# 16-column attention: the down weights loaded one piece per group, and the last two units of a stage turned into the upper bank of their own scores

## The reference

```
# first of the two: inside the block, x is normalised first, no bias
q, k, v = (x @ w_qkv) split into 12 heads of 16
a = softmax(q @ k.T * 0.25)            # 36 x 36 per image and head
o = (a @ v) merged @ w_proj + b_proj
# the later one
a = softmax(q @ k.T * 0.25 + bias); o = (a @ v) merged @ w_proj.T + b_proj
# the stage behind the first is the MLP (w_fc1, gelu, w_fc2);
# the one behind the later is the mixture of experts (w_gate, w_up, w_down; ws_gate, ws_up, ws_down)
```

## Time and profile before

| | |
|---|---|
| median of 3 runs | 899.25 us (898.99 to 905.46) |
| the profiled execution | 903.05 us, its span 901.3 us |
| TensorE busy | 818.9 us, 91% |
| VectorE | 542.0 us, 60% |
| ScalarE | 439.9 us, 49% |
| GpSimd | 408.7 us, 45% |
| mean granted clock of TensorE | 0.961 |

### The profile page before, as it was taken

The page is one execution under the profiler, slowest core; times in us unless marked ns, Lnnn a source line. Parts: engine busy times, 40 slices in busy tenths (PEclk is TensorE's granted clock), DMA queues, the critical chain, the costliest instruction groups (busy, mean ns, idle before and its releaser), DMA issues. The chain is left out here.

```text
span 901.3 us, 21350 instructions
## 1 busy us (share of the span) xinstructions
PE 818.9 (91%) x7767; PEld 733.5 (81%) x7767; DVE 542.0 (60%) x1467; ACT 439.9 (49%) x1094; POOL 408.7 (45%) x489
## 2 busy tenths in 40 slices
PE   9899999999998898987999989888879999999973
PEld 8889998899997676766999976666657899899973
DVE  2235565556665898993763337788966622467645
ACT  0246555555644576763345527566626221355523
POOL 1534444344444544342442236767841455244444
PEclk9999999999999999996999989898979999999996
DMA  9910111111110232225200013623200111333252
GB/s 308 265 51 21 31 27 37 31 32 30 37 37 2 35 67 26 34 22 172 24 1 1 1 27 50 157 47 65 46 3 2 36 60 63 81 99 107 77 170 94
DMA packets 103942, 55.78 MB, mean 62 GB/s; under 512 B 67264, under 2 KB 94512, under 8 KB 103840
## 3 DMA queue, kind: packets, MB, share of 16 engines
q1 hardware_dynamic: 99248, 45.99, 21.2%
q0 software_dynamic: 3792, 7.84, 2.5%
q10 hardware_dynamic: 800, 0.59, 0.2%
HBM read 29.81 MB, written 13.97 MB: 49 GB/s over the span
## 5 line engine op out<-in xcount | busy, mean ns | idle before, releaser
L931 POOL TENSOR_TENSOR attn_prob<-attn_prob,attn_recip 100x432 f32<-100x432 f32 x64 | 58.6, 916 | 67.1 <-DVE attn_recip L1316 66.6
L450 POOL TENSOR_TENSOR attn_prob_x<-attn_prob,attn_recip 100x864 f32<-100x864 f32 x32 | 52.6, 1644 | 52.8 <-DVE attn_recip L759 52.8
L1892 POOL DMA_INDIRECT results<-moe_hid_shared x43 | 41.1, 955 | 58.1 <-ACT moe_hid_shared L2107 58.1
L1602 ACT ACTIVATE mlp_hid<-psum,columns 128x384 f32<-128x384 f32 x72 | 38.1, 580 | 41.4 <-PE psum L96 41.4
L1047 PE MATMUL psum<-ident,attn_prob 100*108 100x100 f32 x256 | 35.5, 264 | 21.4 <-POOL attn_prob L931 12.9
L1047 PEld LDWEIGHTS psum<-ident,attn_prob 100*108 100x108 f32 x256 | 26.1, 138 | 27.2 <-POOL attn_prob L931 18.7
L1064 PEld LDWEIGHTS psum<-attn_prob_t,attn_values 108*49 108x49 f32 (+1 forms) x1024 | 33.7, 132 | 15.5 <-ACT attn_prob_t L1183 6.7
L1176 ACT ACTIVATE attn_prob<-attn_prob 100x432 f32<-100x432 f32 x64 | 36.1, 564 | 19.0 <-POOL attn_prob L938 17.8
L2082 ACT ACTIVATE moe_silu<-psum 128x384 f32<-128x384 f32 x36 | 17.7, 491 | 56.5 <-PE psum L107 56.5
L1064 PE MATMUL psum<-attn_prob_t,attn_values 108*49 108x36 f32 (+1 forms) x1024 | 36.0, 217 | 8.3 <-DMA attn_values<-attn_v_tok 5.0
L1555 PE MATMUL psum<-mlp_w_dn_s,mlp_hid 128*128 128x192 f32 (+2 forms) x306 | 42.6, 290 | 0.0
(11 more groups left out here) (474 smaller groups left out, 2790.5 us busy)
## 6 DMA issues: line engine op xcount, KB each, us to landing
embed_patches<-in_x SPq DMA_DIRECT2D x8, 768.0 KB, 14.5
sorted_rows<-mlp_pad_zeros SPq DMA_DIRECT2D x1, 4214.0 KB, 15.6
moe_hid_shared<-sorted_rows SPq DMA_DIRECT2D x43, 98.0 KB, 2.1
attn_v<-attn_v_tok SPq DMA_DIRECT2D x16, 216.0 KB
attn_values<-attn_v_tok SPq DMA_DIRECT2D x96, 27.0 KB
side_raw_a<-in_w_gu_dram SPq DMA_DIRECT2D x8, 288.0 KB, 3.2
side_raw_b<-in_w_gu_dram SPq DMA_DIRECT2D x16, 144.0 KB, 3.4
h_rows<-results SPq DMA_DIRECT2D x6, 288.0 KB, 5.4
```

The lines of the kernel that those rows point to most:

```text
L450: nc.gpsimd.tensor_tensor(prob_x[k % 2][:, :, :, :], prob[k % 3][:, :, :].rearrange("p h (a n) -> p h a n", a=1) .to_broadcast([QP, HEADS, ...
L931: nc.gpsimd.tensor_tensor(pr, pr, recip[k % 2][:, :].rearrange("p (h a) -> p h a", a=1) .to_broadcast([QP, HEADS, SEQ]), ALU.mult).then_in ...
L1602: nc.scalar.activation(hid_step(n), bank(n % 3)[:, 0:MW], ACT.Gelu, bias=b_up[:, c:c + 1]).then_inc(S["gelu_done"], 1)
L1892: nc.gpsimd.indirect_dma_start(out=results, out_offset=bass.IndirectOffsetOnAxis(ap=x_in[j % x_ring][:, D:D + 1].bitcast(U32), axis=0), in ...
```

## The change

Two edits. First, the down weights are no longer issued together: piece `n` is issued at `j == 3` behind the value loads and the raw loads of group `n + 2`. Second, the turns of units 30 and 31 write to bank 3 and bank 5, the upper one of the two banks that held their own scores, and no longer wait for `z_copied`; `copy_turned` reads from there. Lines below L863 move down by one or two.

```diff
-    turned_ps = bank(6).rearrange("p (g a n) -> p g a n", g=4, a=2)
+    def turned_bank(k):
+        return bank(6) if k < units - 2 else bank(3 + 2 * (k % 2))
@@ sync
             if side and j == 3 and g + 1 < side.steps:
                 side.load_step(sp, g + 1)
-            if side and k == per_group + 2:
-                side.load_down(sp)
+            if side and j == 3 and 2 <= g < 2 + len(side.loads):
+                side.load_down(sp, g - 2)
@@ turn
             if k >= 1:
                 pe.wait_ge(S["turned_copied"], k)
+            if 1 <= k < units - 2:
                 pe.wait_ge(S["z_copied"], k)
             flat = prob[k % 3][:, :, :].rearrange("p h n -> p (h n)")
             for n in range(4):
-                last = nc.tensor.transpose(bank(6)[0:3 * SEQ, n * P:n * P + QP],
+                last = nc.tensor.transpose(turned_bank(k)[0:3 * SEQ, n * P:n * P + QP],
@@ copy_turned
-            nc.scalar.activation(prob_t[k % 2][:, :, :, :], turned_ps[0:3 * SEQ, :, :, 0:SEQ], ACT.Copy
+            nc.scalar.activation(prob_t[k % 2][:, :, :, :], turned_bank(k).rearrange("p (g a n) -> p g a n", g=4, a=2)[0:3 * SEQ, :, :, 0:SEQ], ACT.Copy
@@ SideWeights
-    def load_down(self, sp):
-        for dst, src in self.loads:
-            sp.dma_start(dst, src).then_inc(self.S["down_loaded"], 16)
+    def load_down(self, sp, n):
+        dst, src = self.loads[n]
+        sp.dma_start(dst, src).then_inc(self.S["down_loaded"], 16)
```

## The result

The changed kernel takes **889.91 us** (median of 5 runs, 889.31 to 890.75), the kernel before 899.25 us beside it (5 runs, 898.85 to 905.46). The ratio is 0.9882, with a 95% interval of 0.9853 to 0.991: between 8 and 13 us less. By the medians it is 9.3 us, 1.04%. In a later comparison on another chip it was 890.34 against 898.29 us, 8.0 us or 0.9%, ratio 0.991 [0.9878, 0.9941].

The account below looks back on a forecast made before the run. The prediction took VectorE as the fuller engine, nearly full at 14.76 of 15.70 us ahead of the stall. Its terms, 5.64 + 0.96 + 0.48 = 7.1 us off 899.25, gave 892.2 us, range 888.5 to 896.5.

Parts of the forecast that it names:

- The stall: Last attention stage, group 2: without down weights ahead, the 3.49 us value wait goes, saving VectorE's idle 5.64 us.
- the move from 903.05 to 899.25 us: Whole kernel: sum made against the profiled execution, then moved down by 3.8 us to the median of three runs.
- The other pieces cost nothing: Last stage, down pieces behind groups 3, 4 and 5: issued in SyncE's idle time, 3.4 us of cover at group 4.
- Two turns of attn2: Earlier stage, last two turns: each no longer waits 0.48 us for the copy of z, 0.96 us saved.
- One turn of attn3: Last stage, second of the last two turns: 0.48 us wait for z saved, dummy matmuls behind it only move along.
- The clock case: Rival, earlier stage's tail: shorter pauses may keep TensorE's clock up, up to 3.1 us more, 889.1 us; chance 0.10.
- Given back: Rival, groups behind the removed stall: one more meeting with GpSimd's work costs 2.8 us, 895.0 us; chance 0.16.
- Stays: Rival, group 2: value loads slow for a reason other than down weights, only turns gain, 897.8 us; chance 0.07.
- slower: Rival, groups 4, 5 and 6: down pieces stall their value loads, 9.8 us more than now, 909.1 us; chance 0.04.
- The forecast's own range: Whole kernel: 890 to 894.5 us if the forecast itself holds, chance 0.63, with 0.2% for a median of three.
- the stated cases: Whole kernel: within 1% chance 0.79, faster by over 1% (below 890.3 us) 0.17, slower by over 1% 0.04.

Follow-up runs that it names:

- e3: Changed kernel, but the four down weights of the later stage issued together behind group 2's value loads; 893.52 us, ratio 0.9947 to the kernel before.
- e1: Kernel before with only the down-weights edit, one piece per group, turns as before; 893.94 us, ratio 0.995.
- e11: Changed kernel, but the down weights issued two and two, behind the value loads of groups 2 and 3; 888.84 us in one run.
- e4: Changed kernel, but the four down weights issued together ahead of group 4's value loads; 887.64 us, ratio 0.9885 to the kernel before.
- e2: Kernel before with only the turns edit, down weights still together ahead of group 2's value loads; 894.31 us, ratio 0.9958.
- e9: Kernel before with the down-weights edit and one dummy matmul in attn3 ahead of unit 31's turn, which still waits for z; 889.81 us in one run.
- e6: Changed kernel with dummy matmuls in the three longest pauses of the tails of both attention stages; 887.43 us, ratio 0.9874 to the kernel before.

## Why the prediction was right, and where it was off

- **The stall.** Mechanism right in each step: value loads issued in 7.5 us, no wait, no low clock, and the price is VectorE's idle time (five profiles, of which e3 excludes the nearest rival). In the profiled pair it is 5.9 us against the 5.64 of the sum. Against the medians the term is too large, since the first profile of before had the dearest stall of three: 4.6 us on the mean, and 4.1 by e1. The step that failed is the move from 903.05 to 899.25 us: it lowered the base by 3.8 us but left the terms as they were, though the stall itself was part of those 3.8.
- **The other pieces cost nothing.** Right: no wait at groups 3 to 6, and e11 shows that even two at once are free. In before, e3 and e4 the big loads had all landed (at the latest 11.0, 10.5 and 11.1 us behind their issue) 3.1 to 3.6 us before the nine value loads were through theirs, and the first mixing follows that issue by 1.3 us with a burst ahead (before, e3, e4) and without (group 0); what e3 and e4 show is the time that the burst holds SyncE and stretches the issue of the loads behind it.
- **Two turns of attn2, 0.96 us.** Right: 0.9 us at like clocks.
- **One turn of attn3, 0.48 us.** This is the term that was mis-sized: 1.7 us. The prediction said that the dummy matmuls behind it only move along. They were shortened as well: the stretch at clock 0.50 ended about 3 us sooner, the four dummy matmuls ahead of mixing 31 took 1.56 us instead of 2.77, and 1.2 us of the 1.7 are that. The tail's clock was not looked at for this turn, though it was for attn2. Why the clock comes back sooner stays open.
- **The clock case,** "more than the sum", gave 889.1 us, nearest to what came, and 889.91 lies below the 890.3 for which the forecast gave a chance of 0.17. Its mechanism did not hold where it was put: the second low stretch in attn2's tail is in one profile of before and absent from two. A clock effect of the edit is there, but in the tail of attn3. That the number came so near is luck.
- **Given back:** no. The waits for GpSimd are 12.9 us in 11 places as before, and the slowest normalisation (L1337 now) takes 3178 ns against 3193. In before five of the 18 take over 1 us, the slowest from 658.49 to 661.68, and each ends 0.11 to 0.12 us behind an unbroken run of GpSimd's instructions (here L938 to L2604, to 661.57). The changed kernel has six, the sixth of 1.12 us, and so has before's second profile. **Stays** and **slower** fell with the first row of SyncE's queue.
- **The forecast's own range,** 890 to 894.5, is narrower than the bounds that it names: 3.5 to 6.8 and 0 to 1.4 us off 899.25 give 891.0 to 895.8, before any noise.
- Together: 4.6 + 0.9 + 1.7 = 7.2 us are traced to the edits, the forecast's 7.1 by other terms; that the sums agree is luck. Measured by the medians are 8.0 and 9.3. From mixing 12 to 20 it is 1.4 us less on the mean, but e2, with the stall, took 32.65 us there, and before itself 32.53 to 35.02. Whether the edits have a part in this stays open. So the gain came out at 0.9 and at 1.0% by the medians of two comparisons (0.9 and 1.2% by the ratios), on the edge between two of the stated cases.

## What to carry to other kernels

Put a stall's price by what the fullest engine behind it loses, not by the wait in the profile; but take it from several executions, because the size of a stall differs from execution to execution (5.9 us in one profile here, 3.6 to 4.3 in three others). When a transfer is late, look at how long the issuing queue was held by what stands ahead: big loads one or two at a time between groups of small ones cost nothing here, four at once cost 3.6 to 5.9 us ahead of group 2 and 2.5 ahead of group 3. Before a short pause is costed at its own length, read the clock behind it until the stage ends.

## What the runs showed of the hardware

- One program takes 890.17 to 903.46 us in 29 runs on one chip, 1.5% apart, its mean clock between 0.960 and 0.975, and time and clock go together (correlation -0.84). The profiles of the same program have their stretches at clock 0.50 at other places and of other lengths: in the tail of attn2 before has 6.8 us twice, its second profile 6.8 once, its third 10.2 once. The reason is not shown.
- The same time at low clock had no fixed price: ahead of the wait for GpSimd in the tail of attn3 part of it was swallowed (3.21 us of waiting became 1.83 to 1.89 in e9, e11 and the second profile of the changed kernel), behind it it counted (twelve matmul records in 4.70 us at clock 0.50, 2.45 at 1.00).
- Of four loads of 384 to 768 KB in a row the first two or three issue in 0.5 to 0.7 us each, like one alone or two together, and the last holds SyncE for 2.3 to 4.2 us (in one profile the last two for 1.8 and 1.7). The nine small loads behind them took 9.2 to 11.7 us to issue, those without a burst ahead 7.45 to 8.51. The reason is not shown.
- Dummy matmuls in three pauses of 2.16 to 3.21 us gained 2.9 us of 890 in the tails (e6, by the medians of six runs).
